# Row maxima of the scores from two bf16 parts of q and k, computed in four row groups of TensorE, with a reordered period of 303 parts

## Chip, cores and metric

The kernel runs on 1 core of a Trainium2 chip. The metric is the device time of one execution in microseconds. Before the change it is 2330.1 us (median of 3 runs, 2329.72 to 2337.3).

## What is computed

A batch of 16 sequences of 256 tokens with 128 channels passes four residual blocks, each on a layer norm of its input:

```python
x = x + _L0_attn_a_ref(_layernorm(x, axis=-1), ...)   # gated linear attention: conv, silu, 32 heads, out_proj
x = x + _L0_ffn_ref(_layernorm(x, axis=-1), ...)      # "layer 0": softmax attention, then 8 experts
x = x + _L0_attn_b_ref(_layernorm(x, axis=-1), ...)   # 9 shifted gates
x = x + _L0_ffn_ref(_layernorm(x, axis=-1), ...)      # "layer 1": the same weights as layer 0
```

The change is in the softmax attention of the second and fourth block, 16 heads of 8 channels:

```python
q = (src @ Wq + bq).reshape(B, T, NHEAD, HEAD_DIM)
k = (src @ Wk + bk).reshape(B, T, NHEAD, HEAD_DIM)
scores = jnp.einsum('bqhd,bkhd->bhqk', q, k) * scale
probs = jax.nn.softmax(scores, axis=-1)
out = jnp.einsum('bhqk,bkhd->bqhd', probs, v).reshape(B, T, d)
```

The attention runs 32 times: 16 sequences by two layers.

## The kernel before, in words

**The order of the work.** All work on a sequence is cut into 303 parts, named in the string `PERIOD`. A word such as `smax0.1+2` is part `smax`, layer 0, step 1, for the sequence that is 2 behind the newest. The program walks the string 21 times (16 sequences and a lag of up to 5), and each engine issues its share of every part in that order, without any other scheduler. So in the middle of the run one walk, a *period*, does all the parts of one sequence's worth of work, spread over six sequences that are in flight. Engines wait for each other by semaphores. PSUM has eight banks in two rings of four: ring A (`psA`) for the first block, ring B (`psB`) for the others. A part takes the next banks of its ring, and TensorE waits until their former content is drained.

**Attention in parts.** `q` (step 0 for q, 1 for k): TensorE multiplies (L721), ScalarE adds the bias (L995), GpSimd splits the fp32 result into three bf16 parts (L1446 to L1452), and the sync engine SP stores them in DRAM (L535, L538) and loads them again as `q_stack` and `k_stack`, 72 rows that hold the nine pairs of parts (3 x 3, each 8 channels) for 16 heads (L546, L549). The loads wait until the last `es` of the attention before is done (L543). `smax` (4 steps): TensorE computes the scores of eight heads for 128 queries with contraction over the 72 rows, two heads to a bank, four banks (L739, L741):

```python
e.matmul(t[:, 0:T], q_stack[0:ROW_MAX, h, i * P:(i + 1) * P], k_stack[0:ROW_MAX, h, :], ...)
e.matmul(t[:, T:2 * T], q_stack[0:ROW_MAX, h + 1, i * P:(i + 1) * P], k_stack[0:ROW_MAX, h + 1, :], ...)
```

`rowmax`: VectorE reduces each bank to two columns of maxima (L1261), four reductions to a step. `maxt`: the negated maxima are transposed (L749, L750), copied (L1001) and written by a DMA into row 72 of `q_stack` (L553). `es` (4 steps): the scores again, transposed, with the maximum subtracted by that row (L759, L760); `exps`: exponentials (L1009); `ep`: product with V9, the values of a head and a column of ones (L774); `ocopy`, `tail`: copy, transposes (L784), normalisation, output product (L798, L799) and layer norm. The experts are `up` (L833), `relu`, `down` (L845), `acc` (L1342).

**The first block** near the change: `conv` and `zgate` are TensorE products of L609, `xt` transposes of L632, `weigh` L650 and L654, `sum` transposes of L667 and products of L674, `ssq` products of L685, `outp` 16 products to a step (L699) and on VectorE L1232 to L1237, `gated` on VectorE L1221, `prod` L1213. SP also issues the `lvl` loads (L526), 38 small DMAs for a sequence.

A walk has 8 steps of `smax`: 4 of layer 0 and 4 of layer 1, of different sequences. Products with fp32 operands are recorded as two passes each.

## Time and profile before

| | |
|---|---|
| median of 3 runs | 2330.1 us |
| lowest, highest run | 2329.72, 2337.3 us |
| span of the profiled execution | 2333.7 us (the page gives no time of this execution beyond its span) |
| busy: TensorE, VectorE, ScalarE, GpSimd | 91%, 74%, 62%, 35% |
| mean granted TensorE clock | 0.964 |
| DMA engines, mean busy share of the main queue | 15.4% |

The span runs from the first to the last instruction. The page gives averages; because the program walks the same string again and again, the trace is best read by periods: L1141, once a sequence, starts at 1006.4 us and again at 1139.0 us, and so on every 132 to 134 us from 341 us to 2070 us. What lies before and after is the filling and the emptying of the pipeline. A TensorE row gives a start and a modelled duration; rows overlap, so the time that a product takes from the engine is the step from its start to the next start.

### The profile page before, as it was taken

What the parts mean: (1) busy time and instruction counts of PE and PEld (TensorE: products, weight loads), DVE (VectorE), ACT (ScalarE), POOL (GpSimd) and SP (SyncE); (2) the same over time, 40 slices, a digit from 0 to 9 for tenths busy, and PEclk for the clock granted to TensorE, in tenths of its full rate; (3) what the DMA queues carried; (4) which work ended last, traced back from release to release, by engine and by line L of the source; (5) the groups of instructions that cost most, each with busy time, mean ns of one, the idle gap of its engine ahead of it and who ended that gap; (6) DMA issues with size and microseconds to landing.
All of it is one profiled execution on the core that took longest, in us unless ns stands there. A gap on an engine that the chain in (4) does not pass through costs nothing. (4 is left out here: it accounts for less than half of the span.)

```text
span 2333.7 us, 47546 instructions
## 1 busy us (share of the span) xinstructions
PE 2126.1 (91%) x16832; PEld 1618.6 (69%) x16832; DVE 1719.7 (74%) x4431; ACT 1454.2 (62%) x3113; POOL 819.1 (35%) x1204
## 2 busy tenths in 40 slices
PE   4879889999999999999999999999999999998866
PEld 2556667777777777776777777777777777676544
DVE  6666878787887878787787878788797878755433
ACT  3555657677675766767575766767576676754332
POOL 5212332434343433424333333434333342424131
PEclk9979999999999999999999999999999999998777
DMA  5020112121202112120211212110211212010110
GB/s 152 4 47 10 38 35 47 35 48 29 43 17 45 41 36 50 35 47 8 44 37 37 48 36 48 36 37 15 45 40 36 50 35 45 15 46 21 31 34 5
DMA packets 185820, 88.01 MB, mean 38 GB/s; under 512 B 118297, under 2 KB 179873, under 8 KB 180417
## 3 DMA queue, kind: packets, MB, share of 16 engines
q1 hardware_dynamic: 185584, 84.97, 15.4%
q8 instruction: 136, 2.23, 0.4%
q14 instruction: 100, 0.81, 0.1%
HBM read 51.12 MB, written 33.55 MB: 36 GB/s over the span
## 5 line engine op out<-in xcount | busy, mean ns | idle before, releaser
L1186 DVE SCALAR_TENSOR_TENSOR work<-psA,c_conv_w,work 128x255 f32<-128x255 f32 (+2 forms) x810 | 329.2, 472 | 15.6 <-ACT work L926 14.7
L1261 DVE TENSOR_REDUCE nmax<-psB 128x2 f32<-128x512 f32 x512 | 315.9, 679 | 27.5 <-PE psB L741 27.3
L609 PE MATMUL psA<-xnT_a,c_w_in 128*128 128x256 f32 x1088 | 309.9, 409 | 27.7 <-ACT X L950 15.9
L1213 DVE TENSOR_TENSOR att<-att,QK 128x1024 f32<-128x1024 f32 x192 | 235.4, 1253 | 85.4 <-ACT att L963 85.2
L845 PE MATMUL psB<-c_w,hid 128*128 128x128 f32 x2048 | 280.2, 282 | 7.3 <-ACT pt L1009 5.9
L845 PEld LDWEIGHTS psB<-c_w,hid 128*128 128x128 f32 x2048 | 257.8, 194 | 41.1 <-issue 19.0
L1009 ACT ACTIVATE pt<-psB 128x512 f32<-128x512 f32 x512 | 264.4, 606 | 33.0 <-PE psB L760 33.0
L833 PE MATMUL psB<-x1T,c_w 128*128 128x256 f32 x1024 | 276.6, 398 | 6.2 <-ACT hid L1051 5.4
L963 ACT ACTIVATE att<-psA 128x512 f32<-128x512 f32 x384 | 204.5, 610 | 109.7 <-PE psA L650 83.0
L1032 ACT ACTIVATE hid<-psB,c_b 128x256 f32<-128x256 f32 x496 | 210.8, 484 | 57.8 <-PE psB L833 53.6
L609 PEld LDWEIGHTS psA<-xnT_a,c_w_in 128*128 128x128 f32 x1088 | 194.6, 201 | 72.5 <-ACT X L950 24.1
L1397 POOL TENSOR_SCALAR var_eps<-lnmv 128x2 f32<-128x2 f32 x128 | 28.7, 224 | 600.9 <-DVE lnmv L1070 600.9
L1342 DVE SCALAR_TENSOR_TENSOR ff<-psB,w_e,ff 128x128 f32<-128x128 f32 x512 | 155.2, 344 | 97.9 <-PE psB L845 93.5
L1494 POOL TENSOR_TENSOR own<-X,ccoef 128x512 f32<-128x512 f32 x128 | 147.2, 1155 | 210.1 <-PE psA L674 162.8
L833 PEld LDWEIGHTS psB<-x1T,c_w 128*128 128x128 f32 x1024 | 185.1, 195 | 44.1 <-ACT hid L1051 11.4
L674 PE MATMUL psA<-att,X 128*64 128x128 f32 x3072 | 197.5, 278 | 0.0
L674 PEld LDWEIGHTS psA<-att,X 128*64 128x64 f32 x3072 | 166.4, 137 | 21.5 <-issue 21.5
L926 ACT ACTIVATE work<-psA,conv_b,c_conv_w 128x256 f32<-128x256 f32 x270 | 139.5, 563 | 56.9 <-PE psA L609 56.7
L1221 DVE TENSOR_TENSOR Z<-psA,Z 128x512 f32<-128x512 f32 x128 | 86.4, 685 | 109.5 <-PE psA L674 107.8
L739 PE MATMUL psB<-k_stack,q_stack 72*128 72x256 bf16 x512 | 137.0, 294 | 25.9 <-issue 15.2
L1478 POOL TENSOR_TENSOR O_sb<-O_sb,hid 128x256 f32<-128x256 f32 x128 | 101.6, 794 | 135.5 <-DVE hid L1367 125.8
L774 PE MATMUL psB<-pt,V 128*32 128x256 f32 x2048 | 139.2, 389 | 1.0 <-ACT pt L1009 0.9
(246 smaller groups left out, 4275.1 us busy)
## 6 DMA issues: line engine op xcount, KB each, us to landing
qk_scr<-qparts SPq DMA_DIRECT2D x128, 192.0 KB, 2.5
q_stack<-qk_scr SPq DMA_DIRECT2D x96, 192.0 KB
k_stack<-qk_scr SPq DMA_DIRECT2D x32, 576.0 KB
lvl_scr<-work SPq DMA_DIRECT2D x32, 192.0 KB, 5.2
low<-lvl_scr SPq DMA_DIRECT2D x256, 1.5 KB
c_w_in<-in_in_wT SPq DMA_DIRECT2D x1, 2176.0 KB, 9.3
x<-in_x SPq DMA_DIRECT2D x16, 128.0 KB, 4.4
c_w<-in_W SPq DMA_DIRECT2D x2, 1024.0 KB
```

The lines of the kernel that those rows point to most:

```text
L609: e.matmul(t[:, 0:T], w_in[:, first + j * P:first + (j + 1) * P], xnT_a[:, :], start=True, stop=True).then_inc(filled[b], 1)
L674: m = e.matmul(t[j * HD:(j + 1) * HD, f * P:(f + 1) * P], X[:, s, fc + j * HD:fc + (j + 1) * HD], att[:, 2 * f + j, :], start=False, stop= ...
L833: e.matmul(t[:, 0:T], w_1[:, k, j * P:(j + 1) * P], x1T_b[lay][:, :], start=True, stop=True).then_inc(filled[b], 1)
L845: m = e.matmul(t[:, i * P:(i + 1) * P], hb[:, j, i * P:(i + 1) * P], w_2[:, 2 * k + j, :], start=(j == 0), stop=(j == 1))
L963: e.activation(att[:, :, c:c + 64], t[:, :].rearrange("p (t h) -> p h t", h=HG), ACT.Exp).then_inc(drained[b], 1)
L1009: e.activation(pt_b[a % PTS][:, :, :].rearrange("p h q -> p (h q)"), t[:, :], ACT.Exp, scale=float(AD) ** -0.5).then_inc(drained[b], 1)
L1032: e.activation(hid_b[lay][k % 2][:, j, :], t[:, 0:T], ACT.Relu, bias=b_1[:, 2 * k + j:2 * k + j + 1]).then_inc(drained[b], 1)
L1186: m = e.scalar_tensor_tensor(out=cv[:, back:], in0=t[:, 0:T - back], scalar=conv_w[:, c, tap:tap + 1], in1=cv[:, back:], op0=ALU.mult, op1 ...
L1213: e.tensor_tensor(att[:, :, :], att[:, :, :], bc(QK[:, kq, :], 1, HG), ALU.mult).then_inc(att_done, 1)
L1261: e.tensor_reduce(nmax[:, i, 2 * h2:2 * h2 + 2], t[:, :].rearrange("p (h k) -> p h k", k=T), AX.X, ALU.max).then_inc(drained[b], 1)
L1342: m = e.scalar_tensor_tensor(out=ff[:, i, :], in0=t[:, i * P:(i + 1) * P], scalar=w_e[:, i, k:k + 1], in1=ff[:, i, :], op0=ALU.mult, op1=A ...
L1494: e.tensor_tensor(own_b[k % 2][:, :].rearrange("p (h c) -> p h c", c=HD), X[:, tt, h0 * HD:(h0 + HG) * HD].rearrange("p (h c) -> p h c", c ...
```

## The change

1. **Row maxima from two parts.** `smax` no longer uses `q_stack` and `k_stack`. Two new tiles, `q_max` and `k_max`, hold the first two bf16 parts only: 4 pairs (2 x 2) of 8 channels, 32 rows. The 16 heads are divided over four groups of 32 partitions, four heads each. A step issues its eight products as two rounds of four: each round has one product for each of the row groups 0-31, 32-63, 64-95, 96-127, and each group writes a bank of its own. All four banks must be free before the second round.
2. **Loads.** SP issues eight more DMAs for q and eight for k in each attention (16 partitions x 2 KB each), after the parts are stored and after the last `smax` of the attention before. `smax` waits for these, `es` for the loads of the stacks.
3. **Head order.** Wq, Wk and their biases are laid out on the host with the heads permuted; `es` and `rowmax` look up the place of a head.
4. **Small edits.** V9 is 9 columns wide instead of 32 (one memset less at the start). `outp` adds into the residual tile without the tile `osb`: still three VectorE instructions of the same shapes.
5. **Another order** of the same 303 parts. The lag of all parts still reaches 5.

```diff
+RG = 4
+HPG = NH // RG
+MAXROWS = 4 * AD
+def head_of(g, slot):
+    return 2 * RG * (slot // 2) + 2 * g + slot % 2
+HEADS = [head_of(g, slot) for g in range(RG) for slot in range(HPG)]
+PLACE = [HEADS.index(h) for h in range(NH)]
 PERIOD = """
-load_x0.0+0 tail0.5+3 up0.0+3 ep1.0+4 fn0.0+2 relu0.0+3 ocopy1.0+4 es1.1+4 lvl0.0+1 exps1.1+4 down1.6+5 fn0.1+2
...
+silu0.8+2 place0.0+2 mix1.9+4 rowmax0.2+3 mix1.10+4 smax0.2+3 wexp0.0+2 rowmax0.3+3 weigh0.0+2 experts1.0+5 weigh0.2+2
...
-        osb = sb("osb", [P, NT, HID])
-        V9 = sb("V9", [P, NT, NH, 32])
+        q_max = sb("q_max", [P, HPG, T], BF16)
+        k_max = sb("k_max", [P, HPG, T], BF16)
+        V9 = sb("V9", [P, NT, NH, AD + 1])
 # SP, part q
+                    if u:
+                        e.wait_ge(*full(attn_hop("smax", 3, u - 1), RG - 1))
+                    e.wait_ge(qk_stored[k], (16, 48)[k] * (u + 1))
+                    for half in range(2):
+                        for g in range(RG):
+                            e.dma_start((q_max, k_max)[k][32 * g + 16 * half:32 * g + 16 * half + 16, :, :].rearrange("p s t -> p (s t)"),
+                                        dram(qk_scrd[k], (3 * AD * NH * T * half if k else 0) + HPG * T * g,
+                                             [[NH * T, 2 * AD], [1, HPG * T]])).then_inc(max_loaded[k], 16)
                     e.wait_ge(pool_setup, 2)
                     if u:
                         e.wait_ge(*full(attn_hop("es", 3, u - 1), 3))
-                    e.wait_ge(qk_stored[k], (16, 48)[k] * (u + 1))
 # TensorE, part smax
-                        e.wait_ge(qk_stacked[0], 48 * (au + 1))
-                        e.wait_ge(qk_stacked[1], 16 * (au + 1))
+                        e.wait_ge(max_loaded[0], 2 * RG * 16 * (au + 1))
+                        e.wait_ge(max_loaded[1], 2 * RG * 16 * (au + 1))
                     i = k // 2
...
+                    for v in range(2):
+                        slot = 2 * (k % 2) + v
+                        for g in range(RG):
+                            t, b, u = bank(hop, g)
+                            if v == 0 and u:
+                                e.wait_ge(drained[b], u)
+                            m = e.matmul(t[:, v * T:(v + 1) * T], q_max[32 * g:32 * g + MAXROWS, slot, i * P:(i + 1) * P],
+                                         k_max[32 * g:32 * g + MAXROWS, slot, :], start=True, stop=True)
+                            if v == 1:
+                                m.then_inc(filled[b], 1)
 # TensorE, part ep
-                            m = e.matmul(t[32 * j:32 * j + 32, 0:T], V9[:, kt, 4 * g + j, :], pt[:, j % 2, :],
+                            m = e.matmul(t[32 * j:32 * j + AD + 1, 0:T], V9[:, kt, 4 * g + j, :], pt[:, j % 2, :],
 # VectorE, part rowmax
-                        h2 = 4 * (k % 2) + j
+                        p0 = HPG * j + 2 * (k % 2)
```

**What the order moves, first place: TensorE around the `smax` steps of layer 1**, where the first block's `sum`, `outp` and `ssq` run. Before (the four pairs L739, L741 are a step; here are the last pair of step 0 and the first of step 1, with what stands between):

```order
L739 MATMUL psB<-k_stack,q_stack 128x256
L741 MATMUL psB<-k_stack,q_stack 128x256
L667 MATMUL psA<-c_ident,own 128x128 x4
L674 MATMUL psA<-att,X 64x128 x16
L791 MATMUL psB<-c_ident,ff 128x128
L792 MATMUL psB<-c_ident,ff 128x128
L739 MATMUL psB<-k_stack,q_stack 128x256
L741 MATMUL psB<-k_stack,q_stack 128x256
```

Now, from the first step to the last (L760 is `smax`, L687 and L694 are `sum`, L719 is `outp`, L705 `ssq`, L857 `up`, L629 `conv`):

```order
L760 MATMUL psB<-k_max,q_max 128x256 x8
L687 MATMUL psA<-c_ident,own 128x128 x4
L694 MATMUL psA<-att,X 64x128 x16
L760 MATMUL psB<-k_max,q_max 128x256 x8
L719 MATMUL psA<-c_w_out,Z 128x128 x16
L760 MATMUL psB<-k_max,q_max 128x256 x8
L705 MATMUL psA<-att,ones_f 32x256 x16
L822 MATMUL psB<-c_Wo,attnT 128x128
L823 MATMUL psB<-c_Wo,attnT 128x128
L857 MATMUL psB<-x1T,c_w 128x256 x2
L629 MATMUL psA<-xnT_a,c_w_in 128x256 x2
L760 MATMUL psB<-k_max,q_max 128x256 x8
```

The `outp` products have moved between the second and the third step, and the transposes of `tail` (L791, L792) away from between the first and the second.

**Second place: SP around `q` of layer 1.** Before, the row that stands ahead and the loads of one attention:

```order
L553 DMA q_stack<-maxT 1x16x256
L535 DMA qk_scr<-qparts 128x3x256
L546 DMA q_stack<-qk_scr 24x4096 x3
L538 DMA qk_scr<-qparts 128x3x256 x3
L549 DMA k_stack<-qk_scr 72x4096
```

Now:

```order
L573 DMA q_stack<-maxT 1x16x256
L548 DMA qk_scr<-qparts 128x3x256
L558 DMA q_max<-qk_scr 16x1024 x8
L566 DMA q_stack<-qk_scr 24x4096 x3
L551 DMA qk_scr<-qparts 128x3x256 x3
L558 DMA k_max<-qk_scr 16x1024 x8
L569 DMA k_stack<-qk_scr 72x4096
```

Eight loads stand ahead of each stack's.

**Third place: TensorE ahead of the first `smax` step of layer 0.** Before, the last rows ahead of it; in all 44 rows stand between the k product of this attention (L721) and the step:

```order
L726 MATMUL psB<-c_Wv,srcT 128x128
L727 MATMUL psB<-c_Wv,srcT 128x128
L632 MATMUL psA<-c_ident,work 128x128 x4
L798 MATMUL psB<-c_Wo,attnT 128x128
L799 MATMUL psB<-c_Wo,attnT 128x128
L609 MATMUL psA<-xnT_a,c_w_in 128x256 x2
L739 MATMUL psB<-k_stack,q_stack 128x256
```

Now, where 22 rows stand between the k product (L741 of the new file) and the step (L869 `down`, L857 `up`, L808 transposes of `tail`, L652 `xt`, L629 `zgate`):

```order
L869 MATMUL psB<-c_w,hid_1 128x128 x4
L808 MATMUL psB<-c_ident,O_sb 128x128 x8
L652 MATMUL psA<-c_ident,work 128x128 x4
L629 MATMUL psA<-xnT_a,c_w_in 128x256 x4
L815 MATMUL psB<-c_ident,ff 128x128
L816 MATMUL psB<-c_ident,ff 128x128
L822 MATMUL psB<-c_Wo,attnT 128x128
L823 MATMUL psB<-c_Wo,attnT 128x128
L629 MATMUL psA<-xnT_a,c_w_in 128x256 x2
L760 MATMUL psB<-k_max,q_max 128x256 x8
```

The step has moved nearer to the product that it depends on, and the value product (L726, L727) behind it. The 22 rows are five of `down` (four products each), four of `up`, three of `xt`, three of `conv` or `zgate` with two products and one with four, one of `ep`, and the five rows L808, L815, L816, L822 and L823.

## Rows read from the trace of the kernel before

**Rows 1.** The page, part 1: busy time, share and instructions
```profile
PE 2126.1 (91%) x16832; PEld 1618.6 (69%) x16832; DVE 1719.7 (74%) x4431; ACT 1454.2 (62%) x3113; POOL 819.1 (35%) x1204
```

**Rows 2.** Windows: one period of the middle, and the last two stretches
```profile
core 0: us, PE busy (x) PEld busy (x) DVE busy (x) ACT busy (x) POOL busy (x), PEclk, DMA share, GB/s
...
1006.40:1139.00 132.60, 127.63 (x1052) 98.69 (x1052) 105.60 (x275) 90.32 (x195) 49.29 (x74) 1.00 0.16 38
...
2070.00:2200.00 130.00, 110.48 (x734) 78.50 (x734) 59.62 (x186) 58.01 (x129) 37.20 (x63) 0.82 0.12 32
2200.00:2333.70 133.70, 90.82 (x518) 67.54 (x516) 54.33 (x176) 39.81 (x85) 35.29 (x58) 0.78 0.07 18
```

**Rows 3.** Waits of TensorE in that period, the longest: us in total, times, longest
```profile
PE psA L609 <- ACT X L950: 0.8, 1, 0.8
```

**Rows 4.** Timeline of TensorE, 1126 to 1139 us: start, duration, line, tiles, count
```profile
1126.28 1.97 PE L674 MATMUL psA<-att,X 128*64 128x128 f32 x32
1128.18 0.28 PE L739 MATMUL psB<-k_stack,q_stack 72*128 72x256 bf16 x1
...
1128.95 0.27 PE L741 MATMUL psB<-k_stack,q_stack 72*128 72x256 bf16 x1
1129.06 0.60 PE L667 MATMUL psA<-c_ident,own 128*128 128x128 f32 x4
1129.59 1.97 PE L674 MATMUL psA<-att,X 128*64 128x128 f32 x32
...
1135.63 0.27 PE L741 MATMUL psB<-k_stack,q_stack 72*128 72x256 bf16 x1
1135.84 2.10 PE L685 MATMUL psA<-att,ones_f 128*32 128x256 f32 x32
1137.87 0.28 PE L739 MATMUL psB<-k_stack,q_stack 72*128 72x256 bf16 x1
```

**Rows 5.** Timeline of TensorE: an ordinary fp32 product and `ep` in 32-column tiles
```profile
1017.26 1.03 PE L609 MATMUL psA<-xnT_a,c_w_in 128*128 128x256 f32 x4
...
1019.53 1.07 PE L774 MATMUL psB<-pt,V 128*32 128x256 f32 x16
```

**Rows 6.** Groups by line, weight loads: busy us, mean ns, idle before
```profile
L674 PEld LDWEIGHTS psA<-att,X 128*64 128x64 f32 x3072 | 166.4, 137 | 21.5 <-issue 21.5
...
L741 PEld LDWEIGHTS psB<-k_stack,q_stack 72*128 72x128 bf16 x512 | 53.5, 104 | 10.8 <-issue 1.4
```

**Rows 7.** Timeline of TensorE: 32 passes of `outp`
```profile
1007.37 3.82 PE L699 MATMUL psA<-c_w_out,Z 128*128 128x128 f32 x32
```

**Rows 8.** Timeline of VectorE between two `smax` steps of layer 1
```profile
1129.01 2.47 DVE L1261 TENSOR_REDUCE nmax<-psB 128x2 f32<-128x512 f32 x4
1131.61 0.69 DVE L1221 TENSOR_TENSOR Z<-psA,Z 128x512 f32<-128x512 f32 x1
1132.22 2.47 DVE L1261 TENSOR_REDUCE nmax<-psB 128x2 f32<-128x512 f32 x4
```

**Rows 9.** Timelines of TensorE and GpSimd: k product and its split, layer 0
```profile
1028.39 0.60 PE L721 MATMUL psB<-srcT,c_Wk 128*128 128x256 f32 x2
...
1031.38 0.67 POOL L1452 TENSOR_TENSOR qparts<-qkf,qparts 128x256 bf16<-128x256 f32 x1
```

**Rows 10.** Timeline of SP's queue: small loads, stores of k, load of the k stack
```profile
1036.51 3.59 SPq L526 DMA_DIRECT2D low<-lvl_scr  x5
1040.20 1.48 SPq L538 DMA_DIRECT2D qk_scr<-qparts  x3
1043.73 0.31 SPq L549 DMA_DIRECT2D k_stack<-qk_scr  x1
```

**Rows 11.** Timelines of SP and TensorE near the end: last load, and `smax` behind it
```profile
2261.97 0.32 SPq L549 DMA_DIRECT2D k_stack<-qk_scr  x1
...
2267.21 0.37 PE L739 MATMUL psB<-k_stack,q_stack 72*128 72x256 bf16 x1 [8.59 <-issue]
```

89 lines of the change are left out of this document (41 added, 48 removed).

## The prediction

> **What bounds the kernel.** I read the totals first: TensorE is busy for 91% of the span, VectorE 74%, ScalarE 62% [rows 1]. Totals mix the middle with both ends, so the windows come next, cut where the same instruction comes again for the next sequence. In the period from 1006.4 to 1139.0 us TensorE is busy 127.63 of 132.60 us, VectorE 105.60 and ScalarE 90.32 [rows 2]. The reader should see three things there: TensorE is the bound of the middle; only 5.0 us of a period are left as its idle time; and VectorE has 27 us to spare. The list of TensorE's waits in that period confirms it: its longest is one of 0.8 us [rows 3]. In the last 264 us of the span TensorE is busy 110.48 and 90.82 us of 130.0 and 133.7, at a granted clock of 0.82 and 0.78 [rows 2]: there the sequences wait for their own chain, and a cheaper product is worth little. So a microsecond saved on TensorE counts in the middle, which I take as 14 of the 16 sequences.
>
> **What the change removes.** Durations of rows overlap; what a product costs is the step to the next start. A `smax` step is eight products. From the first start at 1128.18 to the eighth at 1128.95 and on to the next instruction at 1129.06 it takes 0.88 us, so 0.11 us for each product [rows 4]. There are 8 steps in a period: 7.0 us.
>
> **What it puts there.** The trace has no row groups, but it has column groups. An ordinary fp32 pass of 256 columns steps by (1.03 - 0.60) / 2 = 0.215 us, from four passes and two [rows 5, 9]; one alone lasts 0.60 - 0.215 = 0.385. `ep` runs the same passes in four groups of 32 columns: 16 of them in 1.07 us, so (1.07 - 0.385) / 3 = 0.23 us for each *four* [rows 5]. Four groups work side by side there. If four row groups do the same, a step is two rounds of 0.11 us, 0.22 us in place of 0.88.
>
> Weight loads are the unknown. One of `smax` takes 0.104 us [rows 6]. Upper bound: the loads of different row groups go one by one; then eight loads need 0.83 us and nothing is gained. Lower bound: they overlap wholly, 0.22 us. The nearest row is `sum`, two groups of 64 columns: a load there takes 0.137 us [rows 6], and yet 32 passes go in 1.97 us, one every (1.97 - 0.28) / 31 = 0.055 us (0.28 is a single one's duration) [rows 4]. Loads of different groups overlap there, two or three at a time, so I take the lower bound and keep the upper for the range.
>
> **The price of changing tiling.** From the last L741 to `ssq`, which uses 32-column groups, the step is 1135.84 - 1135.63 = 0.21 us where 0.11 is usual [rows 4]: 0.10 us for a change of tiling. Going through TensorE's order of one period, I count 32 changes before and 45 after (some `smax` steps now stand beside `sum` and `ssq`, which had their own change already). 13 x 0.10 = 1.3 us in a period. The Trainium skill (TensorEngine Tiling (Array Packing), Tiling Modes, "Key Properties") speaks against the change here: changing the tiling mode drains the engine. If the whole tail of a product had to run out, which is 0.27 - 0.11 = 0.16 us by [rows 4], the 13 changes would cost 2.1 us and the forecast would be 0.8 x 14 = 11 us later. The row shows less than that, and the row decides.
>
> **The sum.** 8 x (0.88 - 0.22) = 5.3, less 1.3, is 4.0 us in a period; x 14 = 56 us. The span of the profiled execution, 2333.7, becomes about 2278. The median of the runs, 2330.1, lies 3.6 below this span, so I set the forecast at 2330.1 - 56 = **2274 us**.
>
> **Edits costed at nothing.** *The new DMAs*: SP issues 16 more in an attention, at 0.31 us (the k stack) to 0.72 us (3.59 / 5, the small loads) [rows 10], 5 to 12 us, 10 to 23 in a period. SP is not busy for a period as a whole; what counts is whether `smax` waits. From the k product to the end of the split: 1032.05 - 1028.39 = 3.7 us [rows 9]. From the first store to the first load behind it: 1043.73 - 1040.20 = 3.5 [rows 10]. Seven more issues: 2.2 to 5.0. Landing: at least the 2.1 us that the last store needed (1043.73 - 1041.68, [rows 10]), at most the 5.2 us of the k stack's 576 KB (2267.21 - 2261.97, [rows 11]). In all 11.5 to 17.4 us. The cover in layer 0 has shrunk: the 22 rows between the k product and the first step are, at 0.11 us a pass or transpose and 0.215 for a 256-column pass, 5 x 0.88 + 4 x 0.87 + 3 x 0.44 + 5 x 0.87 + 0.9 (`ep`) + 0.9 + 0.7 = 16 us. The middle of the chain fits; its upper end sticks out by 1.4 us. Zero is taken, 1.4 x 14 = 20 us stays for the range. *Queue behind it*: the stacks land up to 5 us later, but `es` comes after four reductions of 2.47 us [rows 8] and the `maxt` DMA. *End of the run*: TensorE waits 8.59 us for the k stack [rows 11]; now seven more issues stand ahead (2.2 to 5.0 us) and a smaller load lands up to 3.1 sooner: minus 1 to plus 5 us once, taken as zero. *V9* narrower: the passes stream the same 256 columns. *`outp`* and *`rowmax`*: the same count and shapes on VectorE. *The memset*: at the start, beside loads.
>
> **The order itself** can't be priced by a row. It can give back at most the 5.0 idle us of a period, and take the same if it is worse. I count it as zero, since nothing in the part of it that I can follow is clearly better or worse. The places checked are the `smax` steps of layer 1. A step now needs all four banks drained, 2.47 us of reductions [rows 8]. Between the first two stand a full `sum`, 0.53 + 1.9 = 2.4 us [rows 4]: wait 0.1 to 0.4. Between the next two, 32 passes of `outp`, (3.82 - 0.28) / 31 x 32 = 3.7 us [rows 7], against two `gated` of 0.6 and 2.47 [rows 8]: no wait. Then `ssq`, 2.0 us [rows 4], and four more rows: no wait.
>
> **Rivals.**
>
> *A. The new order also removes idle time.* Half of the 5.0 us: 2.5 x 14 = 35 us more, 2239 us. For it: VectorE and ScalarE have room [rows 2]. Against: the old order already keeps TensorE at 96%.
>
> *B. The banks become the bound.* The Trainium skill has this as a rule (TensorEngine Tiling (Array Packing), Performance Considerations, "PSUM Bottleneck"): after a fourfold speedup of the products, emptying PSUM may be what limits. The mechanism here needs no page: `smax` steps end when the fourth reduction is done, the second round cannot start before, and while TensorE waits nothing else goes, since it is in order. It decides if each step waits 0.5 us more than now (8 x 0.5 = 4.0). Half of that gives 2302, all of it 2330: no change. For it: 19.8 us of reductions in a period (8 x 2.47), VectorE at 105.6 of a period that shrinks to 128.6. Against: the counts above.
>
> *C. The row groups don't run side by side, and the time goes up.* If each load waits for the product ahead, a step stays at 0.88 us, and the 13 changes of tiling remain: 1.3 x 14 = 18 us more, 2348 us. The point from which it decides: a step over 0.88 - 1.3 / 8 = 0.72 us. For it: the weight loads alone, 0.83 us in a row [rows 6]. Against: `ep` and `sum`.
>
> *D. Part of it.* Steps of 0.5 us, or the DMA chain at its upper end: 2294 to 2312.
>
> **Chances and range.** Forecast, 2255 to 2293: 0.58. A, below 2255: 0.17. D: 0.10. B at its full price, 2312 to 2335: 0.08. C: 0.07. The range of 2236 to 2312 leaves out B's full price, C, and the far end of A, together 0.2. A measurement of this kernel can tell about 0.3%, 7 us, from no change. Faster by more than that: 0.58 + 0.17 + 0.10 + 0.01 = 0.86. Within: 0.07. Slower: 0.07.
>
> **What would show it.** In the profile after: the eight L760 of a step start in two rounds of four, a few ns apart inside a round and 0.11 us between, 0.4 us at most from the instruction ahead to the one behind; the period by the once-a-sequence line is near 129 us instead of 132.6; TensorE still busy over 95% of it; VectorE's busy time in a period unchanged at 105 to 106 us. Rival C would show as starts 0.1 us apart, B as idle time of TensorE ahead of L760 put down to the reductions, the DMA chain as waits ahead of the first step of layer 0 put down to nothing or to a DMA. I am wrong if the period stays above 131 us or falls below 127.

## The result and the profile after

| | before | after |
|---|---|---|
| median | 2329.9 us | 2251.05 us (2249.1 to 2252.42, 4 runs) |
| ratio | 1 | 0.9661, 95% interval 0.9641 to 0.968 |
| span of the profiled execution | 2333.7 us | 2249.8 us |
| mean granted TensorE clock | 0.964 | 0.967 |

The change makes the kernel 79 us faster. The forecast was 2274 us with a range of 2236 to 2312: the time lies inside, 23 us below it. The page of the kernel after, part 1, beside [rows 1]:

```profile
PE 2033.1 (90%) x16832; PEld 1544.7 (69%) x16832; DVE 1781.8 (79%) x4431; ACT 1519.9 (68%) x3173; POOL 922.2 (41%) x1203
```

TensorE has 93 us less of busy time. VectorE and GpSimd have more of it for the same work. ScalarE has 60 instructions more: in the new order it loads its function tables 127 times instead of 67, at 1.283 us each, which is 77 us. In the middle these are eight loads a period for four. No run here shows whether they cost the kernel any time. The window of one period in the middle, beside [rows 2] (duration; busy us and instructions of TensorE, of its weight loads, of VectorE, ScalarE, GpSimd; granted clock; DMA):

```profile
1059.60:1186.70 127.10, 122.07 (x1060) 93.82 (x1052) 110.79 (x274) 94.60 (x200) 57.54 (x75) 1.00 0.21 48
```

The period is 127.1 us for 132.6, and TensorE is still busy 96% of it. The line that comes once a sequence, now L1165, starts at 552.5 and ten sequences later at 1821.9: 126.9 us a period. Before, L1141 went from 606.3 to 1937.4 in ten, 133.1 us. So 6.2 us a period are gone, where I had forecast 4.0.

The timeline of TensorE between two `smax` steps of layer 1, beside [rows 4]:

```profile
1083.39 0.40 PE L760 MATMUL psB<-k_max,q_max 32*128 32x256 bf16 x8
1083.72 0.65 PE L687 MATMUL psA<-c_ident,own 128*128 128x128 f32 x4
1084.30 1.97 PE L694 MATMUL psA<-att,X 128*64 128x128 f32 x32
1086.20 0.54 PE L760 MATMUL psB<-k_max,q_max 32*128 32x256 bf16 x8
1086.67 3.50 PE L719 MATMUL psA<-c_w_out,Z 128*128 128x128 f32 x29
```

A step takes 1083.72 - 1083.39 = 0.33 us up to the next instruction; before it was 0.88. The eight start times of the step at 1090.44 stand 4, 3, 3, 111, 2, 4 and 3 ns apart, so two rounds of four, as forecast. The loads do not hold them up, though one takes 93 ns (the group by line, columns: busy us, mean ns, idle before):

```profile
L760 PEld LDWEIGHTS psB<-k_max,q_max 32*128 32x128 bf16 x1024 | 21.8, 93 | 75.0 <-issue 43.7 <-DVE nmax L1285 16.4 <-ACT hid L1075 10.7
```

So the products do what I said. Yet 8 steps at 0.55 us less are 4.4 us, the additional changes of tiling (between products that use different row or column groups) have to be paid from that, and 6.2 us are gone. Something that I had not counted must have given more than 2 us a period.

### The profile page after: what moved, and what is told of

Read it like the earlier page. It is cut to its first block, busy times and chain, and to the rows that moved or that the text cites. A ratio compares the mean times of both kernels' runs of the same rounds, so it can differ in the third digit from the quotient of the medians.

```text
span 2249.8 us, 48192 instructions
## 1 busy us (share of the span) xinstructions
PE 2033.1 (90%) x16832; PEld 1544.7 (69%) x16832; DVE 1781.8 (79%) x4431; ACT 1519.9 (68%) x3173; POOL 922.2 (41%) x1203
## 4 chain that ended last, share of the span: by engine, by line
PE 64%; DVE 10%; issue 4%; ACT 4%; POOL 2%; DMA 1%; SPq 0%; DVEq 0%; POOLq 0%; ACTq 0%
PE psB L869 10%; PE psB L857 9%; PE psA L694 6%; PE psA L719 5%; PE psB L798 5%; PE psA L629 5%; PE psA L670 3%; DVE nmax L1285 3%; PE psB L783 2%; PE psA L687 2%; PE psA L674 2%; PE psB L784 2%; PE psB L760 2%; PE psA L652 2%; DVE work L1210 1%
## 5 line engine op out<-in xcount | busy, mean ns | idle before, releaser
L629 PE MATMUL psA<-xnT_a,c_w_in 128*128 128x256 f32 x1088 | 297.7, 406 | 19.2 <-DVE work L1210 8.8
L1421 POOL TENSOR_SCALAR var_eps<-lnmv 128x2 f32<-128x2 f32 x128 | 40.4, 316 | 632.7 <-DVE lnmv L1094 631.4
L857 PE MATMUL psB<-x1T,c_w 128*128 128x256 f32 x1024 | 282.6, 399 | 7.2 <-ACT hid L1056 5.8
L869 PE MATMUL psB<-c_w,hid 128*128 128x128 f32 x2048 | 275.0, 282 | 2.1 <-ACT pt L1033 1.9
L869 PEld LDWEIGHTS psB<-c_w,hid 128*128 128x128 f32 x2048 | 258.6, 195 | 20.6 <-issue 8.7
L1237 DVE TENSOR_TENSOR att<-att,QK 128x1024 f32<-128x1024 f32 x192 | 251.2, 1341 | 10.1 <-ACT att L987 9.7
L629 PEld LDWEIGHTS psA<-xnT_a,c_w_in 128*128 128x128 f32 x1088 | 202.1, 201 | 62.7 <-DVE work L1210 15.6
L857 PEld LDWEIGHTS psB<-x1T,c_w 128*128 128x128 f32 x1024 | 180.5, 196 | 52.8 <-ACT hid L1056 16.2
L1516 POOL TENSOR_TENSOR own<-X,ccoef 128x512 f32<-128x512 f32 x128 | 159.1, 1253 | 112.6 <-PE psA L694 64.5
L694 PE MATMUL psA<-att,X 128*64 128x128 f32 x3072 | 199.9, 280 | 0.0
L694 PEld LDWEIGHTS psA<-att,X 128*64 128x64 f32 x3072 | 168.5, 139 | 22.0 <-issue 22.0
L798 PE MATMUL psB<-pt,V 128*9 128x256 f32 x2048 | 135.8, 380 | 4.7 <-ACT pt L1033 4.6
L970 ACT ACTIVATE Z<-psA,c_b_in 128x256 f32<-128x256 f32 x256 | 111.2, 473 | 38.7 <-PE psA L629 38.4
L670 PE MATMUL psA<-high,high_sel 117*128 117x512 bf16 x384 | 126.4, 384 | 11.8 <-DVE Z L1245 9.9
```

What stands on the lines that cost most here:

```text
L629: e.matmul(t[:, 0:T], w_in[:, first + j * P:first + (j + 1) * P], xnT_a[:, :], start=True, stop=True).then_inc(filled[b], 1)
L670: m = e.matmul(bv, sel[0:R_HIGH, :], high_buf[0:R_HIGH, c:c + 64, h0:h0 + HG], start=True, stop=not diag, skip_group_check=True)
L694: m = e.matmul(t[j * HD:(j + 1) * HD, f * P:(f + 1) * P], X[:, s, fc + j * HD:fc + (j + 1) * HD], att[:, 2 * f + j, :], start=False, stop= ...
L798: m = e.matmul(t[32 * j:32 * j + AD + 1, 0:T], V9[:, kt, 4 * g + j, :], pt[:, j % 2, :], start=(kt == 0), stop=(kt == NT - 1), skip_group_ ...
L857: e.matmul(t[:, 0:T], w_1[:, k, j * P:(j + 1) * P], x1T_b[lay][:, :], start=True, stop=True).then_inc(filled[b], 1)
L869: m = e.matmul(t[:, i * P:(i + 1) * P], hb[:, j, i * P:(i + 1) * P], w_2[:, 2 * k + j, :], start=(j == 0), stop=(j == 1))
```

## The experiments

The kernel before ran beside each group of them: medians 2327.4, 2334.2, 2332.6 and 2332.0 us. Ratios are to the kernel before beside it.

### The two halves of the change

**The old order with the row groups** (`e1`): the changed kernel with the old table.

```diff
 PERIOD = """
-silu0.8+2 place0.0+2 mix1.9+4 rowmax0.2+3 mix1.10+4 smax0.2+3 ...
+load_x0.0+0 tail0.5+3 up0.0+3 ep1.0+4 fn0.0+2 relu0.0+3 ...
```

> The changed kernel with the period of 303 parts in the order of before. The forecast's working has the row groups bring 4.0 us of a period and the order nothing; the measured change brought 79 us, 6.2 in a period. Theory 'groups 4.0, order the rest': 2274 us (2268 to 2282), period about 128.9 us. Rival 'the groups bring it all' (the old steps also held waits that go away with them): 2248 to 2256. Rival 'the order is needed' (the eight products at once meet banks that are not drained): above 2290, with TensorE waiting ahead of L760.

Measured: 2365.7 us, ratio 1.0174 (1.0141 to 1.0206): the third case. With cheaper products the old order is *slower* than the kernel before.

**The new order alone** (`e2`): the new table, the row maxima from 72 rows of the stacks as before, no loads into the groups.

```diff
-                    for v in range(2):
-                        slot = 2 * (k % 2) + v
-                        for g in range(RG):
+                    for g in range(RG):
+                        for v in range(2):
+                            place = HPG * g + 2 * (k % 2) + v
...
-                            m = e.matmul(t[:, v * T:(v + 1) * T], q_max[32 * g:32 * g + MAXROWS, slot, i * P:(i + 1) * P],
-                                         k_max[32 * g:32 * g + MAXROWS, slot, :], start=True, stop=True)
+                            m = e.matmul(t[:, v * T:(v + 1) * T], q_stack[0:ROW_MAX, place, i * P:(i + 1) * P],
+                                         k_stack[0:ROW_MAX, place, :], start=True, stop=True)
```

> The changed kernel and its order, but smax again from the stacks of 72 rows, and without the loads of q_max and k_max. If groups and order add up: 2330 - 24 = 2306 us (2300 to 2313). If the groups bring it all: 2325 to 2335. If the new order only fits the short step: over 2335.

Measured: 2268.85 us, ratio 0.9759 (0.9731 to 0.9786). That is faster than all three expectations. The order that I had counted at zero, with the small edits of the change, gives 59 of the 79 us. Its window of one period:

```profile
1069.00:1197.90 128.90, 124.48 (x1054) 98.62 (x1056) 110.26 (x276) 94.57 (x201) 57.04 (x74) 1.00 0.18 39
```

It should be read beside [rows 2]. The period is 3.7 us shorter, but the idle time of TensorE went only from 132.60 - 127.63 = 5.0 to 128.90 - 124.48 = 4.4 us. The rest came out of its *busy* time, with the same products. How a wait hides in busy time shows in the timeline of the kernel before, with one row for each product:

```profile
1068.48 0.27 PE L739 MATMUL psB<-k_stack,q_stack 72*128 72x256 bf16 x1
1068.59 0.27 PE L741 MATMUL psB<-k_stack,q_stack 72*128 72x256 bf16 x1
1068.98 1.29 PE L864 MATMUL psB<-srcT,c_w_mix 128*128 128x256 f32 x4
```

The products step by 0.11 us but are drawn 0.27 us long. L864 starts 0.39 us after the last one, 0.28 late; its row names no idle time, and only 0.12 us lie between end and start. Of each lateness up to 0.16 us counts as busy. Summed by the steps from start to start over one period, the same 68 convolution and gate products take 16.9 us before and 15.2 with the new order, the 64 of `smax` 9.4 and 7.5, the transposes of `xt` 4.5 and 3.6, the exponentials' scores (`es`) 8.3 and 7.5; in the other direction the layer tail takes 1.7 us more and the small gate projection 0.9.

**One row group** (`e7`): as `e2`, but each product reads only the first 32 rows of the stacks, so that all use the same row group. It leaves part products out of the row maxima.

```diff
-                            m = e.matmul(t[:, v * T:(v + 1) * T], q_stack[0:ROW_MAX, place, i * P:(i + 1) * P],
-                                         k_stack[0:ROW_MAX, place, :], start=True, stop=True)
+                            m = e.matmul(t[:, v * T:(v + 1) * T], q_stack[0:MAXROWS, place, i * P:(i + 1) * P],
+                                         k_stack[0:MAXROWS, place, :], start=True, stop=True)
```

> The changed kernel, its order kept, but each row-maximum product reads the first 32 rows of the stacks of nine parts: all eight products of a step use one and the same row group, and the maxima come from q's three parts with k's first part and q's first part with k's second part, so the computation is not the reference's. The loads of the four groups are gone. It keeps the changes of tiling and takes away the running side by side. If the gain of the products is that four groups run at once, each product again takes its 0.11 us of columns, a step 0.88 us, and the time is that of the new order alone, 2268.9, plus the changes of tiling (13 a period at 0.09 us, 14 periods: up to 16 us): 2269 to 2287. If fewer rows by themselves made a product cheap (a shorter weight load), it would stay near the changed kernel, 2251 to 2258.

Measured: 2300.3 us, ratio 0.9858 (0.9839 to 0.9876), some 13 us above the expectation's upper end. The timeline of TensorE, a `smax` step and what follows:

```profile
1112.57 1.04 PE L753 MATMUL psB<-k_stack,q_stack 32*128 32x256 bf16 x8
1113.55 0.66 PE L680 MATMUL psA<-c_ident,own 128*128 128x128 f32 x4
```

The step takes 0.98 us, 0.10 more than `e2`'s, since the next instruction starts 0.198 us after the last product for 0.109: the change back of the tiling. The change into it costs as much: from the last pass of `conv` to a step it is 0.312 us where `e2` has 0.216. Fewer rows make a product no cheaper; only running at once does. Means of ten periods now split the change without a remainder: before 133.1, new order 129.0 (L1159 from 552.5 to 1842.5), with the changes of tiling 130.8 (L1156 from 562.5 to 1870.9), with the groups side by side 126.9. That is -4.1, +1.8 and -3.9 us. Of the 1.8 us, 1.1 stand at the steps themselves, in six changes into the tiling and seven out of it; the rest came elsewhere in the period, and its cause is not shown.

**A full product between the rounds** (`e4`): a product of 128 rows and two columns between the first and the second round of each step, so two more changes of tiling in each.

```diff
                     for v in range(2):
                         slot = 2 * (k % 2) + v
                         for g in range(RG):
+                        if v == 1:
+                            t, b, u = bank(hop, 0)
+                            e.matmul(t[:, T:T + 2], ident_bf[:, :], ident_bf[:, 0:2], start=True, stop=True)
```

> The changed kernel with one product of all 128 rows and 2 columns between the two rounds of each smax step: two more changes of tiling in each step, 16 in a period. At 0.10 us for a change and the short product's own 0.03 to 0.06: +0.23 to 0.27 us in a step, 1.8 to 2.2 in a period, 26 to 31 us in all: 2277 to 2282. If a change of tiling has to run the array dry (0.16 us and more): over 2290. If changes cost nothing here because TensorE has waits to hide them: 2250 to 2258.

Measured: 2272.0 us, ratio 0.9768 (0.974 to 0.9795), 1.3 us a period (128.2 for 126.9) for 16 changes and 8 short products. That is less than any of the forecasts that charge for the changes. All of the 1.3 us on the changes would be 0.08 us each; at the step itself, two changes and the short product take 0.21 us, so about 0.10 a change at most, as I took it. The timeline shows the two rounds torn apart:

```profile
1089.02 0.29 PE L763 MATMUL psB<-k_max,q_max 32*128 32x256 bf16 x4
1089.24 0.18 PE L758 MATMUL psB<-ident_bf 128*128 128x2 bf16 x1
1089.36 0.29 PE L763 MATMUL psB<-k_max,q_max 32*128 32x256 bf16 x4
1089.57 0.66 PE L687 MATMUL psA<-c_ident,own 128*128 128x128 f32 x4
```

**Group by group** (`e3`): the two loops exchanged, so both products of a group are issued in a row.

```diff
-                    for v in range(2):
-                        slot = 2 * (k % 2) + v
-                        for g in range(RG):
+                    for g in range(RG):
+                        for v in range(2):
+                            slot = 2 * (k % 2) + v
```

> The changed kernel, but the eight products of a step are issued group by group (both of row group 0, both of group 1, ...) in place of two rounds of four. If TensorE issues strictly in order, the second product of a group waits for the first and each next group starts beside it: five stretches of 0.11 us in place of two, +0.33 us in a step, 2.6 in a period, about 2290 us. If products may pass each other, or if what counts is when the banks fill (the first bank is ready sooner here), 2245 to 2256.

Measured: 2247.15 us, ratio 0.9663 (0.9633 to 0.9693), the same as the changed kernel. A step lasts as long as before:

```profile
1080.68 0.41 PE L760 MATMUL psB<-k_max,q_max 32*128 32x256 bf16 x8
1081.02 0.66 PE L687 MATMUL psA<-c_ident,own 128*128 128x128 f32 x4
```

0.34 us from the first start to the next instruction. The records of this step show why. The four products that raise a semaphore, the second of each group, start together 0.12 us after the four first ones. So the first product of the next group started ahead of the second of this one, though it was issued behind it, and rounds are not needed in the code.

### Why the old order can't use the cheap products

The windows of 15 us around the first three `smax` steps of layer 0, in the kernel before and in `e1`:

```profile
1056.00:1071.00 15.00, 12.19 (x73) 8.06 (x72) 14.67 (x40) 8.84 (x23) 6.16 (x10) 1.00 0.04 11
```

```profile
1067.60:1082.60 15.00, 11.04 (x70) 6.63 (x68) 13.53 (x41) 8.20 (x20) 6.21 (x10) 1.00 0.05 13
```

VectorE, which "has 27 us to spare" over the period, is busy 14.67 of these 15 us before the change. In `e1` neither engine is full there: the two take turns. The order of VectorE's work before explains it, from the timeline of VectorE, before:

```profile
1062.81 2.48 DVE L1261 TENSOR_REDUCE nmax<-psB 128x2 f32<-128x512 f32 x4
1065.20 0.60 DVE L1074 SCALAR_TENSOR_TENSOR x<-x,lnmv,lnrs 128x128 f32<-128x128 f32 x2
1065.72 4.99 DVE L1261 TENSOR_REDUCE nmax<-psB 128x2 f32<-128x512 f32 x8
```

Twelve reductions stand nearly in a row, 7.5 us, and TensorE's steps between them already waited: the second and third took 1.24 and 1.17 us for 0.88. In the changed kernel two steps of layer 0 stand there, the third comes 13 us later, and VectorE is busy 13.4 of the 15 us from 1137 on; the same view:

```profile
1143.40 2.45 DVE L1285 TENSOR_REDUCE nmax<-psB 128x2 f32<-128x512 f32 x4
1145.76 0.61 DVE L1098 SCALAR_TENSOR_TENSOR src<-x,lnmv,lnrs 128x128 f32<-128x128 f32 x2
1146.29 0.61 DVE L1098 SCALAR_TENSOR_TENSOR x<-x,lnmv,lnrs 128x128 f32<-128x128 f32 x2
1146.81 2.48 DVE L1285 TENSOR_REDUCE nmax<-psB 128x2 f32<-128x512 f32 x4
```

In `e1` the steps take as long as the slow products did: 9.6 us a period from the first start to the next instruction, 9.4 before. A step whose products cost 0.33 us takes 1.29 here (timeline of TensorE, `e1`):

```profile
1096.60 0.28 PE L762 MATMUL psB<-k_max,q_max 32*128 32x256 bf16 x3
1097.58 0.39 PE L762 MATMUL psB<-k_max,q_max 32*128 32x256 bf16 x5 [0.69 <-DVE ff L1368]
1097.89 1.13 PE L631 MATMUL psA<-xnT_a,c_w_in 128*128 128x256 f32 x4
```

The fourth product of the first round waits for the fourth bank, which VectorE still reads for the experts' sum (`ff`), and the four that would finish the banks already free stand behind it.

**Group by group in the old order** (`e8`): `e1` with the exchange of loops of `e3`.

> The old order with the products in four row groups (2365.7 us), but issued group by group, so that a step's first product asks for one bank and not all four banks within its first round. If the loss in the old order comes from the structure in two rounds (the wait for the fourth bank holds the first round back), it goes: 2320 to 2335. If it comes from the reductions on VectorE being the limit in that stretch, whichever product asks first, and from the falls of the granted clock that follow TensorE's waits, the order inside a step changes nothing: 2358 to 2372, with the half-clock stretches still in most periods.

Measured: 2340.5 us, ratio 1.0046 (1.0028 to 1.0063), between the two expectations. In the new order the order of issue is worth nothing, here 25 us: a bank whose two products are done can be reduced while the next is awaited. About half of the 25 us stands in periods at full clock (133.4 us for the only one in `e1`, 132.5 on average in `e8`; 0.9 x 14 = 13); the rest went with the stretches at half clock described below. The idle time of VectorE ahead of its 512 reductions (page, part 5), here of `e8` and of `e1`, falls with it:

```profile
L1287 DVE TENSOR_REDUCE nmax<-psB 128x2 f32<-128x512 f32 x512 | 316.3, 682 | 33.4 <-PE psB L762 31.9
```

```profile
L1287 DVE TENSOR_REDUCE nmax<-psB 128x2 f32<-128x512 f32 x512 | 317.5, 682 | 57.1 <-PE psB L762 57.1
```

**The loads alone in the old order** (`e9`): products from 72 rows of the stacks, group by group, but the 16 loads are issued and waited for.

```diff
                         e.wait_ge(max_loaded[0], 2 * RG * 16 * (au + 1))
                         e.wait_ge(max_loaded[1], 2 * RG * 16 * (au + 1))
+                        e.wait_ge(qk_stacked[0], 48 * (au + 1))
+                        e.wait_ge(qk_stacked[1], 16 * (au + 1))
```

> The old order with the row maxima from 72 rows of the stacks as before the change, but with the 16 loads of q and k into the four groups issued and waited for. It is the kernel before plus loads, the other order of heads, the output written in place and the smaller V9. If the loads (SyncE's queue, DMA traffic ahead of the stacks, the wait before the first step) are what makes the old order slow with row groups: 2345 to 2366. If the loss needs the cheap products (waits of TensorE, then half clock): 2322 to 2336, like the kernel before, and hardly any stretch at half clock in the middle.

Measured: 2339.2 us, ratio 1.0029 (1.0016 to 1.0043), between the two expectations and nearer to the second. All edits but the order and the cheap products cost some 5 to 7 us together: the other order of heads, the output in place, the narrow V9 and the loads. They cost it at the end of the run: a period of the middle is 132.5 us for 133.1, while what follows the ten periods takes 405.8 us for 396.3. That is also why the order's 59 us can't be owed to those edits. And `e8`, which differs from `e9` by the cheap products and by not waiting for the stacks, is not faster: in the old order the row groups are worth nothing at all, in the new one (2268.85 to 2251.05) 18 us with their changes of tiling and loads paid.

**Each product four times** (`e10`), meant to bring a step of `e1` back to 0.88 us:

```diff
-                    for v in range(2):
+                    for rep, v in ((0, 0), (1, 0), (2, 0), (3, 0), (0, 1), (1, 1), (2, 1), (3, 1)):
...
-                            if v == 1:
+                            if v == 1 and rep == 3:
```

> The old order with the row groups, but each product made four times in a row of rounds (same results), so a step has eight rounds of 0.11 us, as long as before the change (0.88 us), and TensorE has as little slack for the reductions as before. Everything else is as in the old order with row groups (2365.7 us). If that kernel loses because TensorE idles between the cheap products and the granted clock then falls to half for stretches, the falls vanish here and the time is near the kernel before plus its changes of tiling: 2325 to 2350. If the loads or the changes of tiling cost the time and not the waits, it stays at 2360 or more, since nothing of either is removed.

Measured: 2426.9 us, ratio 1.0401 (1.0377 to 1.0425). It answers "2360 or more" by its number, yet not by its reason: neither loads nor changes of tiling were added. All four banks are now delivered at the end of eight rounds, and VectorE stands before its reductions (page, part 5, of `e10`) for twice as long as in `e1`:

```profile
L1287 DVE TENSOR_REDUCE nmax<-psB 128x2 f32<-128x512 f32 x512 | 317.9, 683 | 116.8 <-PE psB L762 116.8
```

So it was a poor test of the clock, but a good one of the rounds: products and reductions take turns when a step asks for all banks first and gives all of them last. The granted clock had hardly a stretch at half (6.8 us in all in the middle), so the time was lost by waits.

**The steps spread by hand** (`e12`): `e8` with the second and third step of layer 0 moved in the old table.

```diff
-... rowmax0.0+2 zact0.3+1 xcopy0.5+1 smax0.1+2 conv0.8+1 tap0.8+1 tail1.4+4
-smax0.2+2 lvl0.3+1 lvl0.4+1 lvl0.5+1 rowmax0.1+2 lvl0.6+1 xcopy0.6+1 rowmax0.2+2 mix1.2+3 mix1.3+3 ...
-... mix1.6+3 experts1.0+4 mix1.7+3
+... rowmax0.0+2 zact0.3+1 xcopy0.5+1 conv0.8+1 tap0.8+1 tail1.4+4
+lvl0.3+1 lvl0.4+1 lvl0.5+1 lvl0.6+1 xcopy0.6+1 mix1.2+3 smax0.1+2 rowmax0.1+2 mix1.3+3 ...
+... mix1.6+3 smax0.2+2 rowmax0.2+2 experts1.0+4 mix1.7+3
```

> The kernel of the old order issued group by group (2340.5 us), with two of layer 0's four row-maximum steps and their reductions moved in the order's table: the second from between the first and the third to behind the second product of the layer-1 mix, the third to before that layer's first expert. VectorE's twelve reductions in a row become four, four and four, with other work between. If the old order loses because these reductions stand bunched on VectorE while TensorE waits for their banks, a good part of the waits at this place (some 2.0 us a period beyond the products' own time) goes: 2300 to 2325. If the bunch costs nothing and the gain of the new order comes from elsewhere (the convolution and gate products, the layer-1 steps at the period's end), the time stays within 5 us: 2335 to 2345. If the moved steps collide with the mix products, which take their banks from the same ring, it is slower: 2345 to 2370.

Measured: 2419.6 us, ratio 1.0372 (1.0358 to 1.0387), far above even the collision that I had allowed for. A step takes all four banks of its ring, so the next product of the ring waits until the reductions are through (timeline of TensorE, `e12`):

```profile
1109.74 0.99 PE L762 MATMUL psB<-k_max,q_max 32*128 32x256 bf16 x8
1111.57 0.27 PE L845 MATMUL psB<-c_ident,w_e 128*8 128x128 f32 x1 [0.84 <-DVE nmax L1287]
```

Standing next to the mix and expert products, a step has nothing of the other ring behind it. In the new order gate products of ring A (L629) follow both first steps. The clock was also at half for 133 us of the middle, for 20 in `e8`; at the 0.3 us for each that is found below, this is some 35 of the 79 us between the two, an estimate. Spreading the reductions is therefore not enough, and how much of the 59 us is owed to the relieved bunch, and how much to what stands behind each step, these runs do not settle.

### Granted clock

In the middle, between 330 and 2010 us, the records show stretches at half clock: 20 us in all before, none after and in `e2`, 72 in `e1`, 20 in `e8`, 133 in `e12`. Within one kernel the periods with and without a stretch can be compared. Of the ten periods of the kernel before from 606.3 us on, six have no stretch and last 132.0 to 133.1 us; four have one of 3.4 us and last 133.5 to 134.2, about 1.1 us more. Spread over all ten that is 0.5 us, so a small part of the order's 4.1 us a period is clock. In `e1` a period without is 133.4 us, those with 6.8 us are 135.7 and 136.5, with 13.7 us 137.1. The windows of `e1`, a stretch and the clean period:

```profile
1082.90:1089.70 6.80, 6.80 (x24) 5.81 (x24) 6.06 (x21) 4.53 (x8) 3.19 (x5) 0.50 0.01 2
```

```profile
1697.10:1830.50 133.40, 125.20 (x1052) 94.68 (x1052) 105.27 (x275) 90.38 (x195) 49.38 (x74) 1.00 0.20 45
```

**Filled waits** (`e13`): in all but one step of `e1`, four more products of row group 0 behind the first one.

```diff
+                            if v == 0 and g == 0 and (lay, k) != (1, 0):
+                                for rep in range(4):
+                                    e.matmul(t[:, T:2 * T], q_max[0:MAXROWS, slot, i * P:(i + 1) * P],
+                                             k_max[0:MAXROWS, slot, :], start=True, stop=True)
```

> The kernel of the old order with row groups in two rounds (2365.7 us; 71 us at half clock between 350 and 1910 us), with work added: in each row-maximum step but one, where TensorE stands 0.4 to 1.0 us inside the first round, four more products of row group 0 run behind the first one (4 x 0.11 us, into the half of the bank that the second round writes anyway). They are 28 products more a period, 3.1 us if nothing covered them. If the half-clock stretches follow from TensorE's waits and cost what separates this kernel from the one issued group by group (25 us), the added products remove most of them and the time falls though work was added: 2335 to 2355. If the stretches at half clock are a symptom that costs little, and the waits themselves make the time, the products hide in them: 2360 to 2372. If they lengthen the steps: 2372 to 2410.

Measured: 2366.5 us, ratio 1.0153 (1.013 to 1.0176), as `e1`. 28 products a period more cost nothing, so the waits inside the steps are real and as long as read. But the stretches stayed (61 us for 72), so this run doesn't tell what they are worth; that they come from these waits is not borne out.

### Two versions meant to beat both

The largest waits of TensorE in the period of the kernel after, beside [rows 3]:

```profile
PE psB L822 <- ACT attnT L1038: 1.7, 1, 1.7
PE psA L687 <- issue: 1.3, 2, 1.0
```

**First try** (`e11`), on top of `e3`: ScalarE copies the attention output ahead of two silu pairs, the gate pair goes ahead of the waiting L822, an expert product ahead of the sum.

```diff
-down0.6+3 silu0.5+1 down0.7+3 silu0.6+1 tail1.0+4 ... zgate0.1+1 tail1.1+4
-zact0.5+1 tail1.2+4 zgate0.5+1 zact0.6+1
+down0.6+3 down0.7+3 tail1.0+4 ... zgate0.1+1 tail1.1+4
+silu0.5+1 silu0.6+1 zact0.5+1 zgate0.5+1 tail1.2+4 zact0.6+1
...
-gates0.2+1 sum0.1+2 down1.2+5
+gates0.2+1 down1.2+5 sum0.1+2
```

> A version meant to be better than the changed kernel: products issued group by group (2247.2 us), and the two largest gaps between starts of TensorE's products in a period taken on. At 1.97 us in layer 1's tail, TensorE waits for ScalarE's copy of the transposed attention output, which stands behind two silu pairs: the two silu hops move behind the copy, and the products of one gate pair move ahead of the waiting product. At 1.41 us, behind the small gate projection, the transposing sum waits for its tile: layer 1's expert product moves ahead of it. If these waits stand on the path that sets the period, and TensorE stays the bound: 0.5 to 1.5 us of each for 14 periods, 2215 to 2240. If the waits only move to the next product that needs the same engine's result: 2243 to 2252. If the later silu delays the transposes behind it: up to 2265.

Measured: 2277.0 us, ratio 0.9769 (0.9755 to 0.9783): 30 us lost, more than the worst case allowed for. The timeline of TensorE and the window behind it:

```profile
1018.65 0.27 PE L816 MATMUL psB<-c_ident,ff 128*128 128x128 f32 x1
1021.05 1.36 PE L629 MATMUL psA<-xnT_a,c_w_in 128*128 128x256 f32 x4 [2.13 <-DVE work L1210]
```

```profile
1021.05:1027.80 6.75, 6.71 (x24) 4.74 (x25) 4.85 (x17) 2.33 (x5) 2.32 (x5) 0.56 0.09 23
```

The gate products find their bank occupied until VectorE has done the convolution taps, longer than the wait that they were to fill. And after this gap, 2.40 us from start to start, the clock is 0.56 where after the old gap of 1.97 us at the same place it stayed at 1.00. The gap of 2.40 us stands in all 13 periods of the middle; a stretch at half clock follows it in nine and not in the other four. Such stretches sum to 55 us. From 424 us on, the periods with 6.8 us of one last 130.4 us on average, those without 127.9, and since the gap is in both, the 2.5 us go with the clock.

**Second try** (`e14`): the same with `tail1.2` ahead of `zgate0.5` again.

> The version before (2277.0 us) with its failed move taken back: the gate pair's products stand behind the waiting product of layer 1's tail again, since ahead of it they waited 2.13 us for their bank. Kept are the two silu hops behind ScalarE's copy (there the copy began at 1019.14, 0.6 us after the transposes, and not 1.5 us after them) and the expert product ahead of the transposing sum (gap 0.96 us for 1.41 us). If these gaps stand on the path that sets the period: 1.0 us and 0.45 us less for 14 periods, from 2247 to 2225 to 2237. If the waits only move: 2243 to 2252. If the later silu costs more than the copy gains: up to 2260.

Measured: 2243.0 us (2241.22 to 2247.18), ratio 0.9622 (0.9608 to 0.9635), 0.4% better than the changed kernel and the lowest of all; no stretch at half clock in the middle. Against `e3`, on which it builds (2247.15, 0.9633 to 0.9693), the 4 us are hardly clear of noise, since the intervals touch, though its periods are 126.6 us for 127.0. That is the edge of the case in which the waits only move, and the timeline shows them moving:

```profile
1140.32 0.49 PE L822 MATMUL psB<-c_Wo,attnT 128*128 128x128 f32 x2 [0.66 <-ACT attnT L1038]
1140.64 0.39 PE L823 MATMUL psB<-c_Wo,attnT 128*128 128x128 f32 x2
1141.78 1.13 PE L629 MATMUL psA<-xnT_a,c_w_in 128*128 128x256 f32 x4 [0.75 <-DVE work L1210]
```

L822 waits 0.66 us for 1.7, and right behind it L629 now waits 0.75 us for the same bank that stopped the first try.

## Why the prediction was right in its number and wrong in its reasons

**TensorE bounds the middle.** Right: 96% busy before and after. "VectorE has 27 us to spare" was right for the period and wrong for the place: 14.67 of 15 us busy where three `smax` steps stand.

**The step: 0.88 us to two rounds of 0.11.** Right in kind, and 1.4 us a period too large. It lasts 0.33 us, the change of tiling behind it included, and the loads overlap wholly, as `sum` had suggested. Side by side the groups bring 3.9 us a period, not 5.3. One step of the eight still lasts 1.26 us, as it waits for banks (0.67 and 0.27 us inside it), and part of the rest is met by later waits.

**Changes of tiling: 13 x 0.10 = 1.3 us.** Right at the place: going in costs up to 0.10 us and coming out 0.09, which is 1.1 us a period in `e7`. The whole period grew by 1.8, so 0.7 us came on top at other places. Priced at the whole tail of a product, the changes would cost 0.16 us each and 2.1 in all, more than the 0.09 to 0.10 seen. The rule that I had weighed is that a change of mode drains the engine (the Trainium skill, TensorEngine Tiling (Array Packing), Tiling Modes, "Key Properties"). The trace agrees that a change costs something, but not the whole drawn tail.

**The order, "I count it as zero ... at most the 5.0 idle us of a period".** This is the step that failed. It gave 4.1 us a period, two thirds of the whole; which of its moves gave how much stays open. The bound was read from a view that can't give it: a product is drawn 0.27 us long and steps by 0.11, so small waits count as busy, and idle time fell by 0.5 us only while the period fell by 3.7. I also looked only at the `smax` steps of layer 1, where there is room, and not at layer 0, where twelve reductions stood in a row. Looked at there, [rows 8]'s 2.47 us for four would have given 7.4 us of VectorE against three steps of 0.22.

**Errors that cancelled.** Forecast of a period: 0 for the order, +1.3, -5.3, in all -4.0. Measured: -4.1, +1.8, -3.9, in all -6.2. Over 14 periods that is 87 us; the ends took some back, and 79 are left. The groups, with their changes of tiling paid, gave 2.1 us a period for the 4.0 of the forecast, and an order counted at zero made up for it. That the number lay within the range was luck.

**The DMAs, counted at nothing.** Right in the middle. The timeline of SP in the kernel after:

```profile
1128.07 1.55 SPq L551 DMA_DIRECT2D qk_scr<-qparts  x3
1131.58 3.56 SPq L558 DMA_DIRECT2D k_max<-qk_scr  x8
1135.23 0.33 SPq L569 DMA_DIRECT2D k_stack<-qk_scr  x1
```

The first step of layer 0 starts at 1142.26, 7 us after the last issue; its row names no wait. At the end of the run the step waits 13.72 us where it was 8.59 [rows 11], 5.1 us more, the upper end of the "-1 to +5" that I had taken as zero. I had counted seven issues ahead of k's last load, but not the eight loads of q, which stand ahead of k's store: that store is now issued 7.5 us after the start of the k product, before it was 4.2. The timeline of TensorE:

```profile
2183.72 0.61 PE L760 MATMUL psB<-k_max,q_max 32*128 32x256 bf16 x8 [13.72 <-issue]
```

**VectorE "unchanged at 105 to 106 us".** Wrong: 110.79, and 110.26 already in `e2`, while `e1`, `e8` and `e9`, in the old order, have 105.1 to 106.4. The same instructions last longer: the multiplication of a weighted tile 1.34 us for 1.25, the scaling in the first block's layer norm 0.65 for 0.34 (means of the whole run). GpSimd's busy time rose from 49.3 to 57.5 us too. They fall beside other work in the new order, but what makes them longer is not shown, nor whether it cost time.

**The rivals.** *A*, the order also removes idle time: true in direction, and by more than the 2.5 us that I gave it, but not by idle time. *B*, the banks become the bound: wrong for this change and right for the old order, where the cheap products became waits (`e8` against `e9`) and the rounds made it worse (`e1`). The rule I cited for it is that after a fourfold speedup the emptying of PSUM may limit (the Trainium skill, TensorEngine Tiling (Array Packing), Performance Considerations, "PSUM Bottleneck"). The old order bears it out: its groups gained nothing, while the new order's gained 18 us. *C*, no running side by side: wrong; its time, 2348, is also not what the same row group gives, since `e7` has the order's gain. *D* did not come. Since I counted the order at zero, the 2274 us were in truth a forecast for the groups in the old order, and there 2366 was measured, or 2340 when issued group by group (`e8`).

**"Wrong if the period falls below 127."** It is 126.9. By that mark the prediction failed, though the total lay in the range.

## What to carry to other kernels

Cheaper products on the busiest engine can only be worth what the engines that drain them have free *at that place*: cut windows of some 15 us around each group of the products, not of a period, before pricing. Never bound the gain of a reordering by idle time where instructions are drawn longer than they step; sum the steps from start to start instead. And when a step needs all banks of a ring, issue it bank by bank: that was worth 25 us in the old order and cost nothing in the new. Putting work of the other ring behind it is what `e12` suggests, not what a run isolates.

## What was not expected of the hardware

- The granted clock fell to half for stretches in the middle of a run in which TensorE is over 90% busy. After a gap of 1.97 us from start to start it stayed at full in every period of the kernel after; after one of 2.40 us at the same place (`e11`) it fell in nine periods of 13. In the kernel before it fell six times, and the largest gap in the 8 us ahead was 1.0 us. So the size of one gap doesn't tell whether it falls. At half clock, a pass of 256 fp32 columns steps by 0.427 us for 0.216.
- A period was longer by 0.3 to 0.4 us for each microsecond at half clock in it, not by 0.5: (137.1 - 133.4) / 13.7 = 0.27 in `e1`, (130.4 - 127.9) / 6.8 = 0.37 in `e11`.
- Row groups need no interleaving: issued in pairs, the eight products take 0.34 us, in rounds 0.33. In pairs, a product of a free group starts ahead of one issued earlier whose own group is busy (`e3`).
- Products of 32 rows in one row group step by 0.109 us, as those of 72 rows do; the row count alone changes nothing.
